# Token table instead of sorted rows: gathers by a one-hot table, RMS weights folded into the weights, half of W2 split in place

## The chip, the cores and the metric

The kernel runs on one core of a Trainium2 chip. The metric is the device time of one execution in microseconds (us); lower is better. The engines are TensorE (PE, with its weight loads as PEld), VectorE (DVE), ScalarE (ACT), GpSimd (POOL) and SyncE (SP), which here only issues DMAs.

## The reference

```python
# x (32, 112, 256), ctx (32, 375, 256), all float32; 16 heads of depth 16
x = x + xattn(ctx, ctx, layernorm(x), mask, wq, wk, wv, wo)
x = x + ffn(layernorm(x))
def ffn(x):                                   # 8 experts, hidden size 1024, top-1
    xn = x * rsqrt(mean(x * x) + 1e-6) * rms_w
    scores = softmax(xn @ gate_w.T)
    top1_idx, top1_score = argmax(scores), max(scores)
    for e in range(8):
        h = silu(xn @ W1[e] + b1[e]); ye = h @ W2[e] + b2[e]
        out = where(top1_idx == e, ye, out)
    return out * top1_score
```

## The kernel before

There are 32 batches of 112 query rows. **Attention** is a pipeline over batches. In step s the engines work on batch s (scores and row maxima), s-1 (transposed scores, exponentials, values), s-2 (output projection, residual, statistics of the second layernorm), s-3 (normalised row, gate) and ahead on s+1 and s+2 (context transposed, keys, queries). `run_steps` writes out steps -1 to 3, loops over steps 4 to 29 two at a time, and writes out 30 to 34; every engine has its own copy of this order and meets the others at semaphores.

SP issues all plain DMAs in one queue. In step s, for batch b = s: wait for `scoresT_ready` and `k_spilled`; four loads of `k_stack`; wait for `q_spilled`; four of `q_stack`; `load_batch(b+2)` (two of ctx, one of x); x again for the residual (`x_tail`); the spill of `w2_split`; loads of the next chunks of W1 and W2; the spills of keys and, after `q_parts_ready`, of queries for b+1; the spill of `x1` (batch b-2) to `x1_rows`.

VectorE has in a step four quads of row maxima (`row_maxima`, L1315) and between them, in this order: keys' low halves, division of heads, `centre` (L1338), `queries_stats(b+2)` (L1297, L1299, which waits for x of b+2), normalised queries (L1331), queries' low halves, `add_residual` with the second statistics (L1356 to L1360), context's low halves.

GpSimd has in a step: `split_w1` (L519 to L522: scale a 128x512 chunk by 256, round to float16, keep the remainder), `scale_routed` (L539, L540: the centred row times the RMS weights, once for TensorE and once into `xr_all`; waits for `centre`), `queries_rstd(b+2)` (L507, L509; waits for L1299), `split_w2` (L529 to L532), `residual` (L557), `mask_queries(b+1)` (L550, two), and `routed_factor` (L571, seven operations on 112x1: the layernorm and RMS factors of batch b-2). TensorE transposes `xr_now` (L1049) and makes the gate logits (L1058); ScalarE copies them out (L764).

`arena_a` holds attention's tiles and, after it, all of W2 in two float16 parts; so each split chunk of W2 goes to DRAM (`w2_spill`), and 8 DMAs of 1 MB load it back when attention ends.

**Routing** (from L1418). VectorE runs a chain of 35 links, each waiting for the one before: maximum, softmax, one-hot of the first maximum, ranks and counts by two float32 matmuls (L1137, L1139), a scan over batches, slot of each token, expert of each tile of 128 slots (`tile_expert`). GpSimd makes constants by iota and cast (L605 to L630). Then GpSimd issues 32 indirect DMAs (L636) that scatter the rows of `xr_all` (256 values, score, token number) to `sorted_rows`, which a 4.5 MB DMA had cleared at the start (L389).

**FFN**, 35 tiles of 128 slots: SP loads a tile's sorted rows (L464) and its expert's b2 (L468), PE transposes them (L1152), ACT and DVE split them in two float16 parts, PE computes the hidden layer (L1163, 48 matmuls), ACT applies silu (L831), DVE splits (L1497, L1500), PE computes outputs (L1178, 24 matmuls), DVE adds b2 and the residual (L1510, L1516), for which GpSimd gathered rows of `x1_rows` by token number (L649; the number comes from L1479), and GpSimd scatters the result to the output (L655). PE's order is transpose(t+1), hidden(t), outputs(t-1). Four buffers hold rows; the rows of tile t+4 may be loaded when `out_ready` of tile t has come.

## Time and the profile before

| | |
|---|---|
| median of 3 runs | 1008.66 us (1007.75 to 1008.96) |
| profiled execution, own time | 1013.72 us |
| its span | 1012.0 us |
| PE, PEld busy | 849.3, 612.3 us |
| DVE, ACT, POOL busy | 613.6, 448.0, 523.5 us |
| DMA | 143.72 MB, mean 142 GB/s |

The span is what the trace covers; all times of rows are from its start. A share of busy time is a mean over stages with different limits, so it is read stage by stage. A matmul's end is modelled, and GpSimd's spans are rough.

### The profile page before, as it was taken

How to read it: one execution, taken by the hardware profiler on the slowest of the kernel's cores; microseconds unless marked ns; L12 is line 12 of the kernel's file. 1: busy time of each engine (PE TensorE's matmuls, PEld its weight loads, DVE VectorE, ACT ScalarE, POOL GpSimd, SP SyncE). 2: the span in 40 equal slices, each digit the busy share in tenths (PEclk: the TensorE clock that was granted, in tenths of full speed). 3: DMA queues.
4: the chain of work that ended last, by engine and by line, in shares of the span. 5: the costliest groups of instructions: out<-in, count | busy, mean ns of one | idle time of the engine just before them, and what ended most of it. 6: DMA issues, size and time to landing. Idle time of an engine off the chain costs nothing.

```text
span 1012.0 us, 31886 instructions
## 1 busy us (share of the span) xinstructions
PE 849.3 (84%) x9355; PEld 612.3 (61%) x9356; DVE 613.6 (61%) x1906; ACT 448.0 (44%) x1121; POOL 523.5 (52%) x766
## 2 busy tenths in 40 slices
PE   1789999999999999999999999930089999999995
PEld 0456666666666666666666666610077777778773
DVE  4467777777777777777777777441044444445442
ACT  0235555555555555555555555500033333334331
POOL 0355567567667667667667667436622222232221
PEclk9999999999999999999999999955589999999998
DMA  9746765775775775775775775345222122222210
GB/s 255 184 131 164 188 185 160 179 195 149 185 200 147 187 201 144 185 206 142 189 204 142 187 206 144 76 194 215 87 58 72 59 63 76 58 71 71 66 48 7
DMA packets 124528, 143.72 MB, mean 142 GB/s; under 512 B 13274, under 2 KB 116550, under 8 KB 123464
## 3 DMA queue, kind: packets, MB, share of 16 engines
q1 hardware_dynamic: 119048, 132.15, 48.6%
q0 software_dynamic: 4896, 11.05, 3.4%
q8 instruction: 23, 0.38, 0.2%
q14 instruction: 17, 0.14, 0.0%
q10 hardware_dynamic: 544, 0.00, 0.0%
HBM read 100.10 MB, written 44.89 MB: 143 GB/s over the span
## 4 chain that ended last, share of the span: by engine, by line
PE 32%; issue 18%; SPq 15%; DMA 13%; POOL 12%; DVE 6%; ACT 1%; POOLq 0%; DVEq 0%; ACTq 0%
PE ps L1163 13%; DMA arena_a<-in_x 12%; PE ps L1178 10%; SPq L404 4%; SPq L399 4%; POOL arena_a L550 3%; POOL arena_b L529 3%; POOL arena_b L530 3%; PE ps L980 2%; POOL arena_a L557 2%; POOL arena_b L509 1%; SPq L365 1%; PE ps L994 1%; DVE arena_b L1297 1%; SPq L444 1%
## 5 line engine op out<-in xcount | busy, mean ns | idle before, releaser
L1315 DVE CUSTOM_DVE_ANT_0 arena_a<-ps,arena_a 112x375 bf16<-112x375 f32 x256 | 140.5, 549 | 45.5 <-PE ps L916 38.3
L697 ACT ACTIVATE arena_a<-ps 119x448 f32<-119x448 f32 (+1 forms) x256 | 131.7, 540 | 71.9 <-PE ps L942 71.3
L1163 PE MATMUL ps<-arena_b,w_parts 128*128 128x128 f16 x1680 | 148.5, 227 | 5.3 <-issue 4.3
L938 PE MATMUL ps<-arena_a 128*128 128x448 bf16 x384 | 137.3, 357 | 8.0 <-DVE arena_a L1324 5.9
L1163 PEld LDWEIGHTS ps<-arena_b,w_parts 128*128 x1680 | 118.7, 98 | 37.2 <-issue 11.2
L1315 DVE CUSTOM_DVE_ANT_0 arena_b<-ps,arena_a 112x375 bf16<-112x375 f32 x256 | 139.8, 546 | 0.0
L942 PE MATMUL ps<-arena_a 128*128 128x224 f16 x768 | 136.8, 260 | 0.0
L831 ACT ACTIVATE arena_b<-ps,b_sb 128x128 f32<-128x128 f32 x280 | 79.4, 372 | 113.3 <-PE ps L1163 113.1
L655 POOL DMA_INDIRECT out<-arena_b x35 | 35.6, 1018 | 179.8 <-DVE arena_b L1479 131.2
L1497 DVE TENSOR_SCALAR arena_b<-arena_b 128x512 f16<-128x512 f32 x70 | 30.3, 433 | 129.2 <-ACT arena_b L831 91.4
L1178 PE MATMUL ps<-arena_a,arena_b 128*128 x840 | 97.5, 273 | 4.6 <-DVE arena_b L1500 3.8
L942 PEld LDWEIGHTS ps<-arena_a 128*128 128x128 f16 x768 | 75.4, 98 | 39.9 <-issue 0.8
L1178 PEld LDWEIGHTS ps<-arena_a,arena_b 128*128 128x128 f16 x840 | 79.3, 98 | 17.5 <-issue 6.6
L697 ACT ACTIVATE arena_b<-ps 128x448 f32<-128x448 f32 x128 | 66.1, 541 | 49.2 <-PE ps L942 49.1
L994 PE MATMUL ps<-arena_a,arena_b 128*128 128x256 f16 x576 | 80.8, 278 | 5.3 <-DVE arena_a L1315 4.7
L539 POOL TENSOR_TENSOR arena_b<-arena_b,arena_a 112x256 f32<-112x256 f32 x32 | 20.5, 640 | 124.6 <-DVE arena_b L1338 124.6
L980 PE MATMUL ps<-arena_b,arena_a 128*128 128x375 f16 x384 | 76.3, 339 | 2.0 <-DVE arena_b L1276 1.2
L956 PE MATMUL ps<-arena_a,arena_b 128*17 128x112 f32 (+1 forms) x2048 | 74.0, 261 | 0.0
L550 POOL TENSOR_TENSOR arena_a<-arena_a 128x448 f16<-128x448 f16 x64 | 65.5, 1045 | 0.9 <-ACT arena_a L721 0.8
L994 PEld LDWEIGHTS ps<-arena_a,arena_b 128*128 128x128 f16 x576 | 51.7, 99 | 22.8 <-DVE arena_a L1315 14.6
L1282 DVE SCALAR_TENSOR_TENSOR arena_a<-ps,arena_a 128x375 f16<-128x375 f32 x64 | 39.0, 610 | 42.1 <-ACT arena_a L713 42.1
L916 PE MATMUL ps<-arena_a 32*112 32x375 f16 x512 | 48.6, 368 | 18.6 <-DVE arena_a L1282 10.1
(170 smaller groups left out, 1510.0 us busy)
## 6 DMA issues: line engine op xcount, KB each, us to landing
arena_a<-k_spill SPq DMA_DIRECT2D x128, 192.0 KB, 3.8
arena_b<-in_L_ffn_W SPq DMA_DIRECT2D x64, 256.0 KB, 4.3
arena_a<-q_spill SPq DMA_DIRECT2D x128, 112.0 KB, 4.4
k_spill<-arena_a SPq DMA_DIRECT2D x32, 384.0 KB, 4.7
arena_b<-in_ctx SPq DMA_DIRECT2D x32, 256.0 KB
w_spill<-arena_b SPq DMA_DIRECT2D x32, 256.0 KB, 4.5
arena_a<-w_spill SPq DMA_DIRECT2D x8, 1024.0 KB, 11.7
arena_a<-in_x SPq DMA_DIRECT2D x64, 112.0 KB, 4.6
```

The costliest lines, as they stand in the source:

```text
L550: pool.tensor_tensor(q_parts[par][:, part], q_split[:, part].unsqueeze(2).to_broadcast([P, DT, 2, T]), rows, ALU.mult).then_inc(q_parts_re ...
L697: nc.scalar.activation(probsT[u % PROB_BUFFERS][0:n], scoreT_bank[c][0:n, 0:QUAD * T], ACT.Exp, scale=1.0 / SCALE_SCORES).then_inc(probs_r ...
L831: last = nc.scalar.activation(h_act[:, f, :], ps[:, 1 + 2 * parity + f // 4, (f % 4) * P:(f % 4 + 1) * P], ACT.Silu, bias=b1_sb[:, bass.ds ...
L916: mm = pe.matmul(shared_bank[r][0:T, 0:S], q_parts[par][rows, 0, j, a, :], k_parts[par][rows, 0, j, 0:S], start=True, stop=True)
L938: pe.matmul(bank[:, 0:QUAD * T], mask_keys[:, quad, c, :], max_rows[par].rearrange("p h t -> p (h t)"), start=True, stop=False)
L942: mm = pe.matmul(bank[:, 2 * i * T:2 * (i + 1) * T], k_stack[par][:, r, j, c * P:(c + 1) * P], q_stack[par][:, r, j].rearrange("p a t -> p ...
L956: mm = pe.matmul(out_bank[32 * r:32 * r + VW, quad * T:(quad + 1) * T], v_aug[par][0:n, c, QUAD * quad + r, :], probsT[u % PROB_BUFFERS][0 ...
L980: mm = pe.matmul(proj_bank[j][:, 0:S], wk_parts[:, w_part, k, j * P:(j + 1) * P], ctx_parts[par][:, c_part, k, 0:S], start=k == 0 and n == ...
L994: mm = pe.matmul(bank[:, (c % 2) * D:(c % 2 + 1) * D], ctx_parts[par][:, c_part, k, c * P:(c + 1) * P], wv_parts[:, w_part, k, :], start=k ...
L1163: mm = pe.matmul(ps[:, 1 + 2 * parity + f // 4, (f % 4) * P:(f % 4 + 1) * P], w1_parts[:, w_part, bass.ds(e, 1), k, f * P:(f + 1) * P].rea ...
L1178: mm = pe.matmul(ps[:, 5 + parity, 0:D], h_parts[parity][:, h_part, f, :], w2_parts[:, w_part, bass.ds(e, 1), f, :].rearrange("p o d -> p ...
L1315: nc.vector.tensor_tensor_reduce(out=masked_scores[r % 2], in0=shared_bank[r][0:T, 0:S], in1=mask_bias, scale=-1.0, scalar=3.4e38, op0=ALU ...
```

## The change

Rows. `centre` now writes `row_tile[:, 0:D]` beside x1 in `row_tile[:, D:]`, and SP spills the pair (2 KB a row) in the step of batch b-3 to `rows`, laid out [T, B, 2D]. The sorted rows, the zeros and the scatter are gone: VectorE computes for every tile a list of its 128 tokens, and GpSimd gathers row pairs and scores by it (two indirect DMAs a tile). The list comes from TensorE: for each batch a 112x128 one-hot of the place in the tile, times token and batch number in the tile's column, summed over batches in PSUM. GpSimd's code for the FFN is written out, gather(t) ahead of scatter(t-4).

Factors. The two normalisations become one factor (variance plus a constant, power -0.5), and the RMS weights are multiplied into W1's scale and the gate weights at setup. Half of W2 (batches 0 to 15) is split straight to its place in `arena_w`; the other half is spilled and loaded back in four DMAs. Constants of routing are made by GpSimd inside the pipeline's step 32. SP's loop over steps becomes two (from 5 to 16 and from 17 to 28), GpSimd's too (from 4 to 15 and from 16 to 29).

```diff
-                if st.exists(2):
-                    wait_apart(sp, x1_ready, st.batch(2) + 1, sp_passed)
-                    sp.dma_start(x1_rows[bass.ds(st.batch(2), 1)].rearrange("o t d -> t (o d)"),
-                                 x1[st.parity(2)]).then_inc(x1_spilled[st.parity(2)], 16)
-            run_steps(sp, step)
+                if st.exists(3):
+                    wait_apart(sp, centred_ready, st.batch(3) + 1, sp_passed)
+                    sp.dma_start(rows[:, bass.ds(st.batch(3), 1), :].rearrange("t o d -> t (o d)"),
+                                 row_tile[st.parity(3)]).then_inc(rows_spilled[st.parity(3)], 16)
+            run_steps(sp, step, PEELED_FIRST + 1, DIRECT + 1)
...
-                scale = w_scale.to_broadcast([P, W_CHUNK])
+                scale = w1_scale[:, bass.ds(st.half(0), 1)].to_broadcast([P, W_CHUNK])
...
-                wait_count(pool, w2_spilled, 16 * b)
+                if st.base >= DIRECT:
+                    pool.wait_ge(w2_spilled, 16 * (b - DIRECT + 1))
+                    parts = [w2_split[:, part, :] for part in range(2)]
+                else:
+                    parts = [w2_chunks[:, bass.ds(b, 1), part, :].rearrange("p o n -> p (o n)") for part in range(2)]
...
-                for k, a0, a1, op in ((0, mv2[:, 1:2], eps_ln, ALU.add),
-                                      (1, ln2[:, 0:1], minus_half, ALU.pow),
...
+                pool.tensor_tensor(var2, mv2[:, 1:2], eps_two, ALU.add).then_inc(ln2_var, 1)
+                pool.wait_ge(ln2_var, b + 1)
+                pool.tensor_tensor(ln2, var2, minus_half, ALU.pow).then_inc(ln2_rstd, 1)
...
+                if not st.in_loop and st.base == B:
+                    route_constants()
...
-            for b in range(B):
-                pool.indirect_dma_start(out=sorted_rows, out_offset=bass.IndirectOffsetOnAxis(ap=slot_of[:, b:b + 1], axis=0),
-                                        in_=xr_all[:, b, :], in_offset=None).then_inc(scattered, 16)
...
+            pool.wait_ge(route, R_TOKENS)
+            def gather(t):
+                buffer = t % FFN_UNROLL
+                if t >= FFN_UNROLL:
+                    pool.wait_ge(out_ready, t - FFN_UNROLL + 1)
+                pool.indirect_dma_start(out=xs[buffer], out_offset=None, in_=rows.rearrange("t b d -> (t b) d"),
+                                        in_offset=token(t, 0), bounds_check=B * T - 1, oob_is_err=False
+                                        ).then_inc(xs_loaded[buffer], 16)
+                pool.indirect_dma_start(out=score[buffer], out_offset=None,
+                                        in_=score_rows.rearrange("t (b o) -> (t b) o", o=1),
+                                        in_offset=token(t, 0), bounds_check=B * T - 1, oob_is_err=False
+                                        ).then_inc(score_loaded[buffer], 16)
...
+            for t in range(FFN_TILES + FFN_UNROLL):
+                if t < FFN_TILES:
+                    gather(t)
+                if t >= FFN_UNROLL:
+                    scatter(t - FFN_UNROLL)
...
-                pe.wait_ge(xr_ready, 2 * b + 1)
+                pe.wait_ge(centred_ready, b + 1)
...
+            for b in range(B):
+                pe.wait_ge(places_ready, b + 1)
+                mm = pe.matmul(token_bank[:, 0:2 * FFN_TILES], at_place[:, b, :],
+                               in_tile_of[:, b].rearrange("p s n -> p (s n)"), start=b == 0, stop=b == B - 1)
...
+            link(nc.vector.tensor_tensor(in_tile, tile_base[:, :].unsqueeze(1).to_broadcast([T, B, FFN_TILES]),
+                                         slot_base.unsqueeze(2).to_broadcast([T, B, FFN_TILES]), ALU.is_equal))
+            link(nc.vector.tensor_scalar(in_tile_of[:, :, 0], in_tile, token_no[:, :], None, ALU.mult))
+            link(nc.vector.tensor_tensor(in_tile_of[:, :, 1], in_tile,
+                                         batch_no[:, :].unsqueeze(2).to_broadcast([T, B, FFN_TILES]), ALU.mult))
+            assert done[0] == R_TILES
+            for b in range(B):
+                nc.vector.tensor_scalar(at_place[:, b, :], place_no[:, :], place[:, b:b + 1], None, ALU.is_equal
+                                        ).then_inc(places_ready, 1)
+            dve.wait_ge(tokens_found, 1)
```

VectorE's chain is now 32 links and the 32 masks. `link` increments `route` and waits for it. It reaches the one-hot after 5 links (`R_ONEHOT`), the counts' copy after 6, the tile columns after 22 (`R_TILES`), the token list after 28 (`R_TOKENS`), `tile_expert` after 32 (`N_ROUTE`). TensorE makes counts (two bf16 matmuls) after link 5 and ranks (three) after link 6. The one-hots, counts, masks and columns are bf16. FFN matmuls, their order and the number of tiles are the same.

## Rows read from the trace of the kernel before

**Rows 1.** The page: its first line.

```profile
span 1012.0 us, 31886 instructions
```

**Rows 2.** Windows by stage: busy us per engine, clock, DMA share, GB/s.

```profile
62.00:648.00 586.00, 548.66 (x6474) 375.88 (x6472) 440.56 (x1461) 334.05 (x759) 390.74 (x600) 1.00 0.67 174
...
670.00:735.00 65.00, 3.34 (x9) 1.70 (x8) 13.64 (x46) 0.98 (x3) 36.21 (x48) 0.50 0.54 195
```

**Rows 3.** Chain that ended last, attention: start, us, what; first and last of 19.

```profile
218.80 4.97 DMA arena_a<-in_x
...
561.52 4.87 DMA arena_a<-in_x
```

**Rows 4.** Waits from 100 to 600 us: waiter, releaser, total, times, longest.

```profile
POOL arena_b L539 <- DVE arena_b L1338: 105.7, 26, 4.4
...
DVE arena_b L1297 <- DMA arena_a<-in_x: 39.0, 26, 2.2
...
POOL w_parts L522 <- POOL w_parts L520: 4.8, 26, 0.2
```

**Rows 5.** Timeline of one attention step: start, us, engine, line, operation.

```profile
490.98 0.19 POOL L507 TENSOR_TENSOR arena_b<-arena_b,arena_a 112x1 f32<-112x1 f32 x1 [0.42 <-DVE arena_b L1299]
...
497.75 0.36 SPq L439 DMA_DIRECT2D q_spill<-arena_a  x1
...
504.53 0.33 SPq L369 DMA_DIRECT2D arena_a<-in_x  x1
```

**Rows 6.** Window of one microsecond ahead of the stack loads' flow.

```profile
500.00:501.00 1.00, 1.00 (x9) 0.69 (x9) 1.00 (x5) 0.51 (x2) 0.51 (x2) 1.00 0.55 138
```

**Rows 7.** Timeline of the end of attention.

```profile
664.03 0.82 POOL L571 TENSOR_TENSOR arena_b<-arena_b,arena_a 112x1 f32<-112x1 f32 x2 [1.97 <-DVE arena_b L1360]
...
666.67 0.41 DVE L1338 TENSOR_SCALAR arena_b<-arena_b 112x256 f32<-112x256 f32 x1 [2.78 <-POOL arena_b L571]
...
668.04 0.61 PE L1049 MATMUL ps<-ident,arena_b 112*128 112x112 f32 x2 [3.67 <-POOL arena_b L539]
...
670.04 0.18 ACT L764 ACTIVATE gate_logits<-ps 112x8 f32<-112x8 f32 x1 [1.00 <-PE ps L1058]
```

**Rows 8.** Timeline of routing and of the scatters.

```profile
670.25 0.42 DVE L1418 TENSOR_REDUCE arena_b<-gate_logits 112x32 f32<-112x256 f32 x1 [3.17 <-ACT gate_logits L764]
670.29 0.45 POOL L605 IOTA arena_b<- 128x256 int32 x1 [1.80 <-ACT gate_logits L764]
...
677.38 0.42 DVE L1434 COPY arena_b<-ps 112x256 f32<-112x256 f32 x1 [2.27 <-PE ps L1139]
...
680.67 0.23 DVE L1440 COPY arena_b<-arena_b 128x128 f32<-128x128 f32 x1
680.82 0.28 DVE L1441 TENSOR_TENSOR arena_b<-arena_b 128x128 f32<-128x128 f32 x1
...
686.91 0.17 DVE L1469 TENSOR_SCALAR tile_expert<-arena_b 1x35 int32<-1x35 f32 x1
687.38 1.19 POOL L636 DMA_INDIRECT sorted_rows<-xr_all,slot_of  x1 [13.00 <-DVE tile_expert L1469]
...
726.33 0.94 POOL L636 DMA_INDIRECT sorted_rows<-xr_all,slot_of  x1 [0.30 <-issue]
```

**Rows 9.** Timeline of the start of the FFN.

```profile
734.34 0.69 PE L1152 MATMUL ps<-ident,arena_b 128*128 128x128 f32 x2 [2.63 <-DMA arena_b<-sorted_rows]
...
735.31 5.29 PE L1163 MATMUL ps<-arena_b,w_parts 128*128 128x128 f16 x48 [0.28 <-issue]
```

**Rows 10.** DMA issues: queue, count, KB each, us to landing.

```profile
arena_a<-w_spill SPq DMA_DIRECT2D x8, 1024.0 KB, 11.7
...
arena_b<-x_rows,arena_b POOLq DMA_INDIRECT x35, 2.9
```

**Rows 11.** Timeline of one tile of the FFN.

```profile
974.33 0.48 DVE L1516 SCALAR_TENSOR_TENSOR arena_b<-arena_b 128x256 f32<-128x256 f32 x1
...
981.56 0.38 PE L1152 MATMUL ps<-ident,arena_b 128*128 128x128 f32 x2
```

More of the change, by code:

```diff
@@ L35 @@
 FFN_TILES = (B * T + EXPERTS * (P - 1)) // P
+DIRECT = B // 2
 GROUPS = ((0, 0), (0, 1), (1, 0), (1, 1))
@@ L129, in carve @@
                 n *= d
+            n += n % 2
+            if which == "a" and used["a"] + n > arena_a.shape[1]:
+                which = "b"
             at = used[which]
-            used[which] += n + n % 2
-            assert used[which] <= arena.shape[1]
+            used[which] += n
+            arena = arena_a if which == "a" else arena_b
+            assert used[which] <= arena.shape[1], (which, used)
+            n = 1
+            for d in shape:
+                n *= d
             flat = arena[0:parts, at:at + n]
@@ L204, in build @@
         attT = carve("b", P, DT, T)
-        x1 = [carve("b", T, D) for _ in range(2)]
-        centred = carve("b", T, D)
-        xr_now = carve("b", T, D)
         xrT = carve("b", P, DT, T)
@@ L1412, in over_experts @@
             def over_experts(ap):
[L1413 to L1416 removed]
+                return ap.unsqueeze(1).to_broadcast([T, EXPERTS, B])
             dve.wait_ge(gate_copied, B)
[L1418 to L1419 removed]
```

516 lines of the change are left out of this document (256 added, 260 removed).

## The prediction

> **What bounds the kernel now.** I read the stage windows first [rows 2], then the chain of waits, then timelines of the pieces it names. The span of the profiled execution is 1012.0 us [rows 1], its own time 1013.72, the median of the runs shown 1008.66; I work in the span and carry the difference over to the median unchanged. A difference under 0.2% (2 us) counts as none. There are three stages, each with its own limit.
>
> Attention, to about 648 us: TensorE is busy 548.66 of 586 us [rows 2], yet the chain goes through the load of x. It landed last in 18 steps between 218.80 and 561.52, 342.7 us or 19.04 a step [rows 3]. VectorE waits for x in each of the 26 steps of the window, 39.0 us in all [rows 4], and its third quad of row maxima, on which TensorE waits, stands behind that. One step [rows 5]: GpSimd begins the variance of x at 490.98 and runs without a pause through W2's split, the residual and the masking of queries; SP then issues the query spill at 497.75, the x1 spill, eight stack loads, two context loads and x at 504.53. With the landing (4.87 in one step [rows 3]) this loop of SP, DMA, VectorE and GpSimd closes at 18.9 to 19.1. GpSimd's 4 us wait for the centred rows (105.7 us [rows 4]) lies before that point and limits nothing.
>
> Routing, 670 to 735 us: TensorE does 3.34 us of work in 65, at a granted clock of 0.50 (1.2 GHz) [rows 2]. VectorE routes from 670.25 to 687.08; 32 scatters issue from 687.38, the last at 726.33 [rows 8]; sorted rows are read back and hidden(0) starts at 735.31 [rows 9]. The FFN behind is TensorE's own work and only moves with its start.
>
> **The change, part by part.**
>
> *End of attention.* In the last step the factor took seven GpSimd operations from 664.03, the centring began at 666.67, the first routed transpose at 668.04, the last gate copy ended at 670.22 [rows 7]. Now it takes two operations, the 0.82 us pair of the first row: centring can begin at 664.96, 1.7 earlier. TensorE then reads VectorE's output without the two GpSimd products: centring ends 0.41 after its start, so 0.96 us lay between, and about 0.15 remains. Together 2.5: routing starts at 667.75.
>
> *Route constants.* 36 GpSimd operations enter the first step after the last split. A 256-element iota takes 0.45 and its cast begins 0.52 after it [rows 8]; at 0.2 to 0.5 each I estimate 12 us. GpSimd's products and five factor operations have gone, and VectorE and TensorE are busy there with batches 30 and 31; factor and residual of those are needed about 13 us on. I cost it at nothing. If it were 5 us longer, the centring of batch 30 and with it the tail would be 3 us late.
>
> *VectorE's chain to the token table* (R_TOKENS, 28 links). A 256-element link costs 0.42 + 0.04, a small one 0.17 + 0.03 [rows 8]. Five links to the one-hot 2.3. TensorE's two counting matmuls, in bf16: the old float32 pair left VectorE idle 2.27 [rows 8], a bare handover costs some 0.3; nearer the low end, since the passes are fewer, 0.85. Copy 0.46. Ranks, three longer matmuls in the same bounds: 1.3. Tiles, starts and slots: three at 0.2, two at 0.25, three at 0.46, 2.5. Slot to tile: 0.9. Three operations over 1120 elements a partition: 0.17 plus 1.05 ns an element (the slope between the 1x35 and 112x256 links) is 1.35; 1.38 with the link for the two with two tensors, 0.8 for the scalar one (0.75 to 1.38). Then 32 place masks of 128 elements, each with its own matmul: the nearest row is the 128-element copy, after which the next operation starts 0.15 later [rows 8], so 4.8, plus 0.3 for the last matmul; bounds 0.11 (3.5 in all) and 0.5 (16). Six small ones 1.3. The sum 18.2 against 16.8 before: the table is ready at 686.0. The four links that follow (expert of each tile) and the scores' way out hide behind the gathers.
>
> The Trainium skill ("VectorE: DVE Perf Modes", What auto-detection actually checks) says that a one-source operation on 16-bit tensors in SBUF runs in the 4x mode. No row here shows a bf16 pair; by that rule masks come at the lower spacing, and the time would be about 2 us less than by the row.
>
> *Scatter and read-back go, gathers come.* GpSimd starts 0.30 after its release, and further indirect DMAs follow 1.25 to 1.35 apart [rows 8]. Hidden(0) stands behind transpose(1), whose rows are the third indirect DMA (rows 0, score 0, rows 1): 686.3 + 2.6 = 688.9. A gather lands in 2.9 [rows 10]; 2 KB rows for 1 KB, +0.3: 692.1. Then 0.97 as before [rows 9]: hidden(0) at 693.1, against 735.31: 42.2 us earlier, the 2.5 included. Bounds of this sum: 37 (both matmul waits 2.27, scalar operations at one element a cycle) to 46. Two waits are new: SP waits for the scores (ready some 4.5 us into VectorE's chain) with the W2 reload and the b2 loads queued behind, and GpSimd for the scores' spill with the gathers behind; both are over some 10 us before the table. The W2 reload is four 1 MB transfers instead of eight, issued before the table; eight landed in 11.7 us each at the median [rows 10], and outputs(0) needs them only some 9 us after hidden(0). Nothing.
>
> *FFN.* GpSimd has three indirect DMAs a tile, some 4 us of a period of 7.4. The gather of a tile is released by the output four tiles back, ready at 974.81; the transposes that would need it come a tile later, at 981.56 [rows 11]. With 0.14 + 1.0 + 3.2 it lands with 2.4 us left. VectorE loses 0.15 us a tile that hides under TensorE. Nothing; without the cover each microsecond of lateness would cost 31.
>
> *The attention loop.* Removed: two products, five factor operations, 16 W2 spills. None is in the cycle: the spill is issued behind x on SP, the products stand before the wait. So no gain. Three things lengthen it. (1) In the direct steps the split writes to an address from a register: the like store of W1 waits 4.8/26 = 0.18 us [rows 4], W2's store is too short of a wait to be in that list: +0.1 in 12 looped steps, 1.2 (0 to 2.2). (2) The row spill is 224 KB for 112, queued between query spill and stack loads. In the microsecond before the loads flow, DMA is 0.55 busy [rows 6], so most fits into the gap; 112 KB at that row's 138 GB/s is 0.8 us, less the idle 0.45: at most some 0.4, at least 0. I take 0.1 in 29 steps, 2.9. (3) SP has two loops to enter instead of one. 0.5.
>
> The Trainium skill ("Runtime: NRT & Kernel Launch", Instruction fetch mechanics) says a taken branch out of the fetched window stalls the engine. No row above isolates it; it gives no figure for a loop entry.
>
> *Setup.* Two small VectorE operations ahead of the weights, 0.4, less one 112 KB broadcast; the 4.5 MB of zeros goes, on which nothing critical waited. +0.2.
>
> Sum: -42.2 + 1.2 + 2.9 + 0.5 + 0.2 = -37.4. Span 974.6; median 1008.66 - 37.4 = 971.3.
>
> **Rivals.**
> A. The cycle of x takes the full 0.4 to 0.5 us a step, through the doubled spill and its 64 KB stride: 29 x 0.35 more, 981.5. For it: no slack on that path [rows 3]. Against: the gap [rows 6].
> B. The table is slow: mask, semaphore and matmul pair at 0.3 to 0.5 us instead of 0.15, 5 to 11 more: 976 to 982. For it: 32 handovers at TensorE's lower clock. Against: VectorE doesn't wait between them.
> C. The bf16 operations run at the fast end (masks 3.5, long ones halved: -3.8) and the loop loses nothing (-4.6): 963.
> D. Slower than before: the loop stretches. The saving of 42 is used up when each of 29 steps is over 1.45 us longer, for instance if the strided row writes took 0.3 us each instead of fitting the gap (7 to an engine). Time then 1012 and up. Against: the 1 KB W2 spill writes have strides of the same kind, and end within the step.
> E. No change: row gathers late in every tile by 1.2 us. Speaks against it the 2.4 us left.
>
> **Chances.** Forecast 0.69 (its own range 966 to 977), A 0.10, B 0.08, C 0.10, D 0.02, E 0.01. Range 963 to 982: it takes in C, A and most of B. Faster 0.97, same 0.01, slower 0.02.
>
> **What would show it.** Two GpSimd operations and one centring between the last statistics and the last transposes, and the last gate copy some 7 us after those statistics instead of 9; VectorE's chain from the first routing operation to the last token operation 18 us (17 to 21); 32 masks 0.15 apart; first gather 0.3 behind; hidden(0) 25 us after the last gate copy; then 277 us to the end, as before. Steps of 19.0 to 19.3 in the loop. The prediction is wrong if the steps move by over 0.3 either way, if the table is nearer 30 us, or if TensorE waits for gathered rows in the loop of tiles.

## The result, and the profile after

The changed kernel takes 973.47 us at the median of four runs (972.89 to 974.91), the kernel before 1008.4 on the same chip: ratio 0.9656, 95% interval 0.9639 to 0.9673, 34.9 us less. On a second chip the medians are 973.46 and 1010.22, ratio 0.9636 (0.9614 to 0.9658). The prediction was 971.3, in the range 963 to 982.

That the total came out near the forecast is luck: it hides errors of opposite sign. The stages up to the last gate copy became 8.0 us shorter where 2.3 longer was forecast, those behind it 32.7 shorter where 39.7 was forecast. Each kernel was profiled twice; the stages are read from the starts of the score matmuls, the last gate copy, hidden(0) and the last output in the timelines (us, first and second trace; the difference is that of the means):

| stage | before | after | difference | predicted |
|---|---|---|---|---|
| start to step 5 | 136.5, 138.0 | 133.3, 135.0 | -3.1 | +0.2 |
| steps 5 to 31 | 495.1, 495.5 | 492.0, 492.5 | -3.0 | +4.6 (29 steps, entry) |
| step 31 to the last gate copy | 38.7, 38.4 | 36.9, 36.5 | -1.9 | -2.5 |
| last gate copy to hidden(0) | 65.1, 64.4 | 27.5, 27.5 | -37.3 | -39.7 |
| hidden(0) to the last output | 266.2, 266.1 | 270.8, 270.4 | +4.4 | 0 |
| last output to the end | 10.4, 10.4 | 10.6, 10.6 | +0.2 | 0 |

The traces differ by 40.7 us, the medians by 35 to 37, since both profiled executions of the kernel before were 3 to 5 us over its medians (1013.72 to 1008.4, 1014.69 to 1011.83), those of the kernel after within 1 (972.89 and 974.21). In each of four sets of its runs, the executions with a listed mean clock of 0.955 and more were on average 1.4 to 2.2 us longer than the rest, and both profiled ones (0.957 and 0.958) are of that kind; what else makes up the 3 to 5 us is open. The first line of the page after, for [rows 1]:

```profile
span 971.1 us, 31136 instructions
```

The windows after, for [rows 2]: busy us per engine, clock, DMA share, GB/s:

```profile
62.00:640.00 578.00, 544.61 (x6433) 372.19 (x6431) 436.82 (x1455) 332.64 (x754) 310.00 (x395) 1.00 0.66 174
662.00:690.00 28.00, 8.08 (x45) 4.80 (x46) 18.15 (x67) 1.36 (x4) 7.55 (x8) 0.50 0.52 188
```

GpSimd has lost some 80 us of work in attention and TensorE is as busy as before; routing is 28 us for 65, still at a granted clock of 0.50, the lower level. The end of attention, for [rows 7]:

```profile
658.58 0.19 POOL L583 TENSOR_TENSOR arena_b<-arena_b,arena_w 112x1 f32<-112x1 f32 x1 [5.87 <-DVE arena_b L1400]
658.85 0.56 POOL L585 TENSOR_TENSOR arena_b<-arena_b,arena_w 112x1 f32<-112x1 f32 x1
...
659.44 0.41 DVE L1378 TENSOR_SCALAR arena_w<-arena_w,arena_b 112x256 f32<-112x256 f32 x1 [1.00 <-POOL arena_b L585]
...
660.00 0.61 PE L1071 MATMUL ps<-ident,arena_w 112*128 112x112 f32 x2 [1.08 <-DVE arena_w L1378]
...
662.00 0.18 ACT L786 ACTIVATE gate_logits<-ps 112x8 f32<-112x8 f32 x1 [1.00 <-PE ps L1080]
```

Two GpSimd operations, the centring 0.86 us behind the start of the first (2.64 in [rows 7]), TensorE 0.15 behind the centring's end, as forecast. Routing and the first gathers, for [rows 8, 9]:

```profile
662.22 0.42 DVE L1457 TENSOR_REDUCE arena_b<-gate_logits 112x32 f32<-112x256 f32 x1 [2.36 <-ACT gate_logits L786]
...
665.41 0.39 DVE L1466 CAST arena_b<-ps 128x224 bf16<-128x224 f32 x1 [0.59 <-PE ps L1160]
...
670.34 1.33 DVE L1489 TENSOR_TENSOR arena_b<-tile_base,arena_b 112x1120 bf16<-112x1120 bf16 x1
671.70 0.53 DVE L1491 TENSOR_SCALAR arena_b<-arena_b,token_no 112x1120 bf16<-112x1120 bf16 x1
...
673.62 0.58 DVE L1496 TENSOR_SCALAR arena_b<-place_no,arena_b 112x128 bf16<-112x128 bf16 x3
...
680.38 0.20 DVE L1507 SCALAR_TENSOR_TENSOR arena_b<-arena_b 128x35 uint32<-128x35 f32 x1
...
681.63 1.29 POOL L676 DMA_INDIRECT arena_b<-rows,arena_b  x1 [17.91 <-DVE arena_b L1511]
...
684.53 1.00 POOL L676 DMA_INDIRECT arena_b<-rows,arena_b  x1 [0.30 <-issue]
...
688.72 0.69 PE L1187 MATMUL ps<-ident,arena_b 128*128 128x128 f32 x2 [2.52 <-DMA arena_b<-rows,arena_b]
...
689.69 4.33 PE L1198 MATMUL ps<-arena_b,w_parts 128*128 128x128 f16 x48 [0.28 <-issue]
```

VectorE's chain to the table took 18.36 us (662.22 to 680.58; 18.2 forecast), the 32 masks 5.3. The first gather begins 1.05 us behind the table, not 0.30, and the transposes of rows(1) start 4.2 after their gather, not 3.2. The DMA issues, for [rows 10]:

```profile
arena_w<-w_spill SPq DMA_DIRECT2D x4, 1024.0 KB, 8.1
arena_b<-rows,arena_b POOLq DMA_INDIRECT x35, 3.5
```

### The profile page after: what moved, and what is told of

It is laid out like the page before. It is cut to its first block, busy times and chain, and to the rows that moved or that the text cites. A ratio compares the mean times of both kernels' runs of the same rounds, so it can differ in the third digit from the quotient of the medians.

```text
span 971.1 us, 31136 instructions
## 1 busy us (share of the span) xinstructions
PE 851.8 (88%) x9388; PEld 610.6 (63%) x9389; DVE 619.2 (64%) x1895; ACT 449.1 (46%) x1122; POOL 453.0 (47%) x564
## 4 chain that ended last, share of the span: by engine, by line
PE 47%; POOL 11%; DMA 10%; SPq 10%; issue 10%; DVE 9%; ACT 2%; POOLq 0%; DVEq 0%; ACTq 0%
PE ps L1198 14%; PE ps L1213 10%; DMA arena_w<-in_x 9%; POOL arena_w L570 4%; PE ps L1002 3%; SPq L443 3%; PE ps L1016 3%; SPq L438 3%; PE ps L960 3%; PE ps L978 2%; PE ps L964 2%; POOL arena_b L558 2%; PE ps L938 2%; POOL arena_w L559 2%; POOL arena_w L577 1%
## 5 line engine op out<-in xcount | busy, mean ns | idle before, releaser
L719 ACT ACTIVATE arena_b<-ps 128x448 f32<-128x448 f32 (+1 forms) x384 | 194.2, 541 | 119.6 <-PE ps L964 118.8
L1356 DVE CUSTOM_DVE_ANT_0 arena_w<-ps,arena_w 112x375 bf16<-112x375 f32 x256 | 140.3, 548 | 48.7 <-PE ps L938 42.1
L960 PE MATMUL ps<-arena_b,arena_w 128*128 128x448 bf16 x384 | 137.2, 357 | 6.2 <-DVE arena_b L1365 5.6
L1356 DVE CUSTOM_DVE_ANT_0 arena_b<-ps,arena_w 112x375 bf16<-112x375 f32 x256 | 139.5, 545 | 0.1
L964 PE MATMUL ps<-arena_b 128*128 128x224 f16 x768 | 136.7, 260 | 0.0
L1213 PE MATMUL ps<-arena_w,arena_b 128*128 x840 | 97.7, 273 | 4.8 <-DVE arena_b L1536 3.4
L978 PE MATMUL ps<-arena_b 128*17 128x112 f32 (+1 forms) x3072 | 100.4, 261 | 0.3
L1213 PEld LDWEIGHTS ps<-arena_w,arena_b 128*128 128x128 f16 x840 | 78.9, 98 | 18.6 <-issue 7.1
L1016 PE MATMUL ps<-arena_w,arena_b 128*128 128x256 f16 x576 | 80.8, 278 | 4.3 <-DVE arena_w L1356 3.4
L1002 PE MATMUL ps<-arena_b,arena_w 128*128 128x375 f16 x384 | 75.6, 337 | 2.0 <-DVE arena_b L1317 1.2
L1016 PEld LDWEIGHTS ps<-arena_w,arena_b 128*128 128x128 f16 x576 | 51.7, 99 | 21.2 <-DVE arena_w L1356 13.5
```

The source lines that it names most:

```text
L719: nc.scalar.activation(probsT[u % PROB_BUFFERS][0:n], scoreT_bank[c][0:n, 0:QUAD * T], ACT.Exp, scale=1.0 / SCALE_SCORES).then_inc(probs_r ...
L960: pe.matmul(bank[:, 0:QUAD * T], mask_keys[:, quad, c, :], max_rows[par].rearrange("p h t -> p (h t)"), start=True, stop=False)
L964: mm = pe.matmul(bank[:, 2 * i * T:2 * (i + 1) * T], k_stack[par][:, r, j, c * P:(c + 1) * P], q_stack[par][:, r, j].rearrange("p a t -> p ...
L978: mm = pe.matmul(out_bank[32 * r:32 * r + VW, quad * T:(quad + 1) * T], v_aug[par][0:n, c, QUAD * quad + r, :], probsT[u % PROB_BUFFERS][0 ...
L1002: mm = pe.matmul(proj_bank[j][:, 0:S], wk_parts[:, w_part, k, j * P:(j + 1) * P], ctx_parts[par][:, c_part, k, 0:S], start=k == 0 and n == ...
L1016: mm = pe.matmul(bank[:, (c % 2) * D:(c % 2 + 1) * D], ctx_parts[par][:, c_part, k, c * P:(c + 1) * P], wv_parts[:, w_part, k, :], start=k ...
```

## The experiments

All ratios are to the kernel before, timed beside them; its medians there lay between 1010.2 and 1011.8. The diffs show the lines that matter; "..." marks what is left out. Where a step or a stage is given, it is read from the profiled execution.

**A second trace of before.** No edit.

> The kernel before, profiled a second time. Its first profiled execution had an own time of 1013.72 us, 5 above the median 1008.4. If those 5 us lay in the stretch before the first step's scores and in the steps of the second half (theory: the trace of before was a long one there), this trace shows step 16 starting about 344 instead of 347 us and step 31 about 628 instead of 631.5, and the loop gained little by the change. Rival: this execution takes 1008 and is as long as the first one in the steps (19.0 in both halves), and the 5 us lay elsewhere.

1014.69 us in the profiled run. Step 5 starts at 138.0, steps 5 to 16 take 19.14 on average, 17 to 28 19.06: as in the first trace, and step 16 starts at 348.5, not at 344. The rival holds in what it says of the steps: the first trace was no freak there, and the changed kernel's second half (18.79) is really shorter. Its 1008 us didn't come: this execution too is over the median.

**Zeros put back.**

```diff
+            sp.dma_start(sorted_rows.rearrange("(n p) d -> p n d", p=P),
+                         zeros.unsqueeze(1).to_broadcast([P, FFN_TILES, D + 2])).then_inc(zeroed, 16)
...
+            pool.memset(zeros, 0.0).then_inc(constants, 1)
```

> The kernel after with the 4.5 MB write of zeros put back where it was (its result is not used). Theory 1: that write competed with the loads of the first steps; step 1's scores start about 59.5 instead of 56.7 us, and the time is 976 to 976.5, some 2.8 above 973.5. Theory 2 (my prediction's): nothing critical waits for it, the first step's 2.8 us come from elsewhere; 973.5, within 0.5.

975.68 us, ratio 0.9651 (0.9625 to 0.9677); step 1 starts at 57.3 (56.7 and 58.8 in the two traces of the kernel after), so the write costs nothing at the start, as predicted. But in the steps 17 to 28 it took 18.95 for 18.79, and GpSimd's subtraction of the split 1160 ns for 1090. The tile `zeros` had moved the tiles behind it by 1032 bytes. Whether the one follows from the other, this run doesn't show; it led to the sweep below.

**Seven GpSimd operations put back.**

```diff
+                for n in range(5):
...
+                    pool.tensor_tensor(spare_row[:, n:n + 1], eps_two, eps_ln, ALU.add).then_inc(spare, 1)
+                for n in range(2):
...
+                    pool.tensor_tensor(spare_row, bvo, bvo, ALU.mult).then_inc(spare, 1)
```

> The kernel after with seven GpSimd operations of the sizes of the removed ones put behind the factor in each step (five of one column, two of 112x256; their results are not used). Theory: their removal shortened the loop's GpSimd chain or took load off the port that VectorE shares; with them the steps behind the direct half go back from 18.7 to 19.0, the direct half from 19.1 to 19.3, and the time is 977 to 980. Rival (the prediction's 'none is in the cycle'): steps unchanged, the tail at most 3 us later, 973.5 to 976.

974.59 us, ratio 0.963 (0.961 to 0.965), steps 17 to 28 18.83. The rival holds, the prediction's "none is in the cycle": the removed products and factors gave the loop nothing that stands out from the difference between two traces of one kernel.

**Half the row spill.** The centred halves in DRAM are filled once, with x, so the FFN computes on other numbers with the same instructions.

```diff
+            sp.dma_start(rows[:, :, 0:D], x.rearrange("b t d -> t b d")).then_inc(filled, 16)
...
-                    sp.dma_start(rows[:, bass.ds(st.batch(3), 1), :].rearrange("t o d -> t (o d)"),
-                                 row_tile[st.parity(3)]).then_inc(rows_spilled[st.parity(3)], 16)
+                    sp.dma_start(rows[:, bass.ds(st.batch(3), 1), D:].rearrange("t o d -> t (o d)"),
+                                 row_tile[st.parity(3)][:, D:]).then_inc(rows_spilled[st.parity(3)], 16)
```

> The kernel after with a row spill of the residual half alone, 112 KB a step instead of 224; the centred halves of the rows in DRAM are filled once, during the first steps, with x (the FFN's input is replaced by x). My prediction put 0.1 us a step on the doubled spill: then 2.9 us less than the kernel after, 970.6, or a ratio to before of 0.963, and steps 0.1 shorter in both halves. Rival A of the prediction: 0.4 to 0.5 a step, 0.952. Theory 3: the doubled spill fits the gap before the stack loads and costs nothing: ratio 0.9656, steps as in the kernel after (19.16 on average over steps 5 to 16, 18.8 over 17 to 28).

Steps 5 to 16 took 19.06 (19.16 and 19.25 in the two traces of the kernel after), 17 to 28 18.68 (18.79, 18.78). The 0.1 of the prediction agrees, though two traces of one kernel differ by as much in the first of these; rival A is out. Its total (973.08, 0.961) says little: the four executions took 970.0, 970.9, 975.2 and 977.2, and the longest, the profiled one, has an FFN 5 us longer than the kernel after's.

**All of W2 through the spill.**

```diff
-DIRECT = B // 2
+DIRECT = 0
...
-            run_steps(sp, step, PEELED_FIRST + 1, DIRECT + 1)
+            run_steps(sp, step)
```

> The kernel after with the direct half at nothing: all of W2 goes through the spill, 8 reload transfers instead of 4. Each tile that GpSimd touches keeps its position within 64 bytes. Theory P: the direct split costs 0.1 us of GpSimd's path a step (6.65 against 6.55 from the variance to the masked queries) and 0.35 of the period; without it steps 5 to 16 fall from 19.16 to 18.8, like those behind them, and the last gate copy is 4 us earlier. The reload then has only some 25 us from its issue at 660 to outputs(0): 8 MB at the 200 GB/s that the loads move take 40, and outputs(0) waits about 15 us for them, so that the whole is slower than the kernel after, 985. Rival: steps unchanged, so the half without W2 spills differs for another reason; and reload in time, 973.

981.84 us, ratio 0.9702 (0.9675 to 0.9729). GpSimd's path from the variance to the masked queries is 6.54 us in every step, as theory P says (6.65 in the direct half of the kernel after), but the steps take 19.12 and 19.14, so theory P's price for the direct half is wrong, at least as this run tests it: the edit also takes SP's and GpSimd's loops back to their one entry, so that the second half (18.79 before the edit) changed by it too. Outputs(0) did not wait for the reload: it starts 10.0 us behind hidden(0) in both. The reload held up the rows instead. Window of the gathers in this kernel:

```profile
684.00:697.00 13.00, 1.93 (x10) 1.14 (x11) 2.91 (x11) 0.77 (x2) 8.28 (x8) 0.50 0.99 385
```

With the DMA engines at 0.99, rows(1) took 6.5 us from gather to transposes for 4.2, and hidden(0) came 2.3 later. This is what the direct half gives here.

**No score gathers.** The outputs are scaled with a column of the identity.

```diff
-                pool.indirect_dma_start(out=score[buffer], out_offset=None,
-                                        in_=score_rows.rearrange("t (b o) -> (t b) o", o=1), ...
...
-                nc.vector.scalar_tensor_tensor(out=out_rows[buffer], in0=y_sb, scalar=score[buffer],
+                nc.vector.scalar_tensor_tensor(out=out_rows[buffer], in0=y_sb, scalar=ident[:, 0:1],
```

> The kernel after without the 35 score gathers (the outputs are scaled by a column of the identity instead of the score). Theory S: the third indirect DMA of each tile is what makes three of four tiles 0.2 us longer than before (it delays the loading of TensorE's instructions or the reading of the expert number); from hidden(0) to the end 276.7 as in the kernel before, and rows(1) come 1.3 earlier: ratio 0.9596, some 6 us less than the kernel after. Rival W: TensorE's new addressing of W2 costs it; then the tiles stay at 281.4, and only the 1.3 us are won, 972.

970.02 us, ratio 0.9592 (0.9562 to 0.9622). Theory S falls: from hidden(0) to the last output 270.2, as in the kernel after (270.8, 270.4). What was won lies behind the last output (7.8 us for 10.6), where no engine computes any more. The 1.3 us were not won either: rows(1), gathered second instead of third, landed 5.9 us after their gather.

**A gather ahead, and a sweep of tile positions.** One execution, 1061.38 us with the sweep behind the last output.

```diff
...
+            pool.indirect_dma_start(out=warm_row, out_offset=None, in_=rows.rearrange("t b d -> (t b) d"), ...
...
+            for moved in range(3):
+                for shift in range(0, 16, 2):
+                    at.shift = [shift if k == moved else 0 for k in range(3)]
+                    then(pool.tensor_tensor(at(2, D, T), at(0, D, T), at(1, D, T), ALU.add))
```

> The kernel after with two additions. (1) One indirect gather of rows 0 to 127, not used, on GpSimd while the token table is made. Theory: the first indirect DMA after a long pause loads GpSimd's code, which is why the first gather came 1.05 us after the table and not 0.30; then the first real gather comes 0.3 behind and hidden(0) 0.75 earlier. Rival: 1.05 is what a gather's release costs, unchanged. (2) Behind the last output, a sweep: GpSimd's split subtraction, residual addition and query masking, each 24 times, with one operand at a time moved by 8 bytes over 64. Theory B: the durations that changed between the kernels (subtraction 1158 to 1090 ns, masks 1045 to 977, residual 638 to 729) follow from the tiles' positions; the sweep shows the same steps of about 70 and 90 ns. Rival: position does nothing (all within 10 ns) and the durations changed by what ran beside them. The span is about 75 us longer by the sweep.

The first real gather starts 0.88 after the table for 1.05 and takes 1.01 us for 1.29, so 0.45 of the delay has to do with its being the first; the rest stays. Later releases cost less: in the loop of tiles GpSimd starts a gather 0.80 us behind the output that frees its buffer. Hidden(0) gained nothing (27.6 behind the last gate copy): rows(1) took 4.7 from their gather. The sweep, six single operations of its timeline: subtraction, addition, masking, each with both sources at multiples of 16 bytes, then with one source 8 bytes further:

```profile
976.10 1.15 POOL L726 TENSOR_TENSOR arena_w<-arena_w 128x512 f16<-128x512 f32 x1
977.34 1.08 POOL L726 TENSOR_TENSOR arena_w<-arena_w 128x512 f16<-128x512 f32 x1
1005.41 0.72 POOL L730 TENSOR_TENSOR arena_w<-arena_w 112x256 f32<-112x256 f32 x1
1006.21 0.64 POOL L730 TENSOR_TENSOR arena_w<-arena_w 112x256 f32<-112x256 f32 x1
1032.93 1.04 POOL L734 TENSOR_TENSOR arena_w<-arena_w 128x448 f16<-128x448 f16 x1
1034.05 0.98 POOL L734 TENSOR_TENSOR arena_w<-arena_w 128x448 f16<-128x448 f16 x1
```

Moving on by 8 bytes each time alternates between the two: the subtraction 1152, 1081, 1153, 1092, 1152, 1090, 1152, 1092 ns with its first source moved, the addition 723, 641, 723, 640, 723, 640, 722, 638 (635 to 639 with the second moved), the masking 1042, 977, 1038, 973, 1040, 975, 1038, 972 with its second. The other source, moved in its turn, changes nothing for the subtraction (1152 to 1155) and the masking (1037 to 1044), and nor does the output (within 3 ns). Theory B holds.

**The kernel after again**, as the base for the last versions.

> The kernel after, unchanged, on the same chip as the three that follow and as a second trace of it: 973.5 us, or a ratio of 0.963 to 0.966; from the last gate copy to hidden(0) 27.5 us, from there to the last output 270.8, steps 19.2 in the direct half and 18.8 behind it.

As expected in every stage (table above); its start to step 5 took 1.7 us more than in the first trace.

**W1 in the order of W2.**

```diff
-        w1_parts = sb("w1_parts", [P, 2, EXPERTS, DT, F], F16)
+        w1_parts = sb("w1_parts", [P, EXPERTS, 4, 2, W_CHUNK], F16)
...
-                                           w1_parts[:, w_part, bass.ds(e, 1), k, f * P:(f + 1) * P
+                                           w1_parts[:, bass.ds(e, 1), 2 * k + f // 4, w_part, f % 4 * P:(f % 4 + 1) * P
```

> The kernel after with W1 stored in the same order as W2 (expert, chunk, part), nothing else. With one order for both the adds come back: tiles of 7.06, from hidden(0) to the last output 4 to 5 us less, 969. Rival: the gather queue or VectorE sets the 7.24, nothing changes, 973.5.

967.25 us, ratio 0.959 (0.9568 to 0.9611), 6.2 less than the kernel after. Hidden(0) to the last output 267.5. The chains that ended last, one tile each, of the kernel after and of this one:

```profile
757.52 4.18 PE ps L1198 x48
761.71 2.78 PE ps L1213 x24
764.49 0.22 PE ps L1187 x2
764.71 0.13 issue
764.84 4.18 PE ps L1198 x48
```

```profile
784.87 4.07 PE ps L1198 x48
788.94 2.76 PE ps L1213 x24
791.70 0.22 PE ps L1187 x2
791.92 3.11 PE ps L1198 x36
```

The matmuls are the same; the 0.13 "issue" between transposes and hidden units is gone. Of the loop's four kinds of tile two last 7.06 to 7.15 us for 7.25 to 7.37, one 8.33 for 8.51, one is as it was. In the trace of TensorE's sequencer the outputs of four tiles have 48 ALU_OP and 16 FUSED_REGOPS for their addresses in the kernel before, 64 FUSED_REGOPS in the kernel after, and 48 and 16 again here. Theory W holds for 3 of the 4.4 us; the rest of the 6.2 lies ahead of the FFN.

**A version meant to beat both.** Beside the W1 order:

```diff
-                    for n, (w_part, h_part) in enumerate(PASSES):
-                        mm = pe.matmul(ps[:, 5 + parity, 0:D], h_parts[parity][:, h_part, f, :],
+                    for h_part in ((1, 0) if f == FT - 1 else (0, 1)):
+                        n = D if h_part else 2 * D
+                        mm = pe.matmul(ps[:, 5 + parity, 0:n], h_parts[parity][:, h_part, f, :],
+                                       w2_parts[:, bass.ds(e, 1), f, 0:n].rearrange("p o d -> p (o d)"),
...
-            transpose_rows(1, 1, 0, False)
-            hidden(0, expert_of(0), 0, True)
+            hidden(0, expert_of(0), 0, True, lambda: transpose_rows(1, 1, 0, False))
...
+        carve("a", T, 2)
```

> A version meant to beat both. On the kernel after: (1) the two parts of a W2 row side by side, so that one address serves both and the high part of the hidden units is multiplied with 512 columns at once: 16 matmuls and 8 addresses for the outputs of a tile instead of 24 and 16; VectorE adds the two halves; W1 in the same order; (2) hidden(0) begins ahead of the transposes of tile 1, which come in its middle; rows of tiles 0 to 2 are gathered ahead of the scores; Silu's table is loaded during the routing; (3) two words of padding that put the residual's two sources 8 bytes apart. If TensorE's sequencer is what bounds the FFN, as its trace says (32 addresses x 0.124 + 16 x 0.124 + 1.2 for the expert's number and the waits = 7.2), a tile falls to about 6.2 and the FFN by 28 to 31; (2) gives 3 to 4, (3) 0.09 a step, 1 to 2.5: 936 to 942. If TensorE's array bounds it, only (2) and (3) show: 968.

949.1 us, ratio 0.9395 (0.9379 to 0.9412): 24 less than the kernel after, though not the 936 to 942 expected. FFN 253.3 for 270.6, last gate copy to hidden(0) 25.1 for 27.5, residual 637 ns for 729, steps 17 to 28 18.68. Two tiles of its chain:

```profile
784.98 3.39 PE ps L1224 x48
788.37 2.74 PE ps L1240 x16
791.11 0.22 PE ps L1211 x2
791.33 0.38 issue
791.71 4.21 PE ps L1224 x48
795.92 0.09 issue
796.01 2.77 PE ps L1240 x16
```

In every other tile the 48 matmuls of the hidden units now run in 3.4 us instead of 4.2; the others start behind 0.4 to 0.6 us of issue and still take 4.2. In the 3.4 us tiles the sequencer's first address stands 0.7 us ahead of the first matmul, in the others 0.1. The outputs stay at 2.7 us with 16 matmuls as with 24, for the same number of columns, so no instruction bound them.

The sequencer has lost its lead by a wait. It worked out its last address at 803.04 and passed the wait for gathered rows only at 804.95, 0.03 us behind their landing, and those rows had been asked for late:

```profile
800.04 0.48 DVE L1583 SCALAR_TENSOR_TENSOR arena_b<-arena_b 128x256 f32<-128x256 f32 x1 [0.24 <-DVE arena_b L1576]
...
801.33 1.02 POOL L689 DMA_INDIRECT arena_b<-rows,arena_b  x1 [4.02 <-DVE arena_b L1583]
...
805.04 0.44 PE L1211 MATMUL ps<-ident,arena_b 128*128 128x128 f32 x2
```

The output frees the buffer at 800.52, the gather starts 0.80 later, and its rows are there 3.6 us behind that. Such stands of 1.4 to 2.0 us come in every fourth tile, and in 18 of the 28 tiles from 4 to 31 the sequencer passes that wait within 0.05 us of the landing; in the kernel after it comes 0.9 to 2.6 us behind it. So the gathers with their four buffers bind this version beside the sequencer. That fits a gain of 17 instead of 28; a version with more buffers, which would show it, was not run.

**SP's loop one step later, in the kernel before.**

```diff
...
-            run_steps(sp, step)
+            run_steps(sp, step, PEELED_FIRST + 1)
```

> The kernel before, with SP's loop of two steps entered one step later, as the change had to do it for its two loops; the work is the same. The trace of before shows 0.32 us more between query spill and key loads in every second step, where SP's loop branches back; the change moved that to the other kind of step. Theory SP: with the branch in the odd steps x is in time there; steps fall from 19.05 to 18.8, 1008 becomes 1001. Rival: no change, 1008, and the 0.25 us a step that the kernel after gains in its second half comes from GpSimd's shorter operations (tile positions) alone.

1008.95 us, ratio 0.9989 (0.9974 to 1.0003), steps 17 to 28 19.03. The 0.32 us more moved with the loop's entry to the other kind of step. The steps 17 to 28 stayed; the steps 5 to 16 took 18.99 for 19.15 and 19.14, and from step 5 to 31 this trace is 3.0 us shorter than those of the kernel before. Theory SP falls with its 7 us; 1 to 3 us are not excluded.

**Padding alone, in the kernel before.** Three lines, 24 bytes a partition.

```diff
...
+        carve("a", P, 2)
         pair_keep = carve("a", P, 2, T)
+        carve("a", P, 2)
...
         w_scale = carve("b", P, 1)
+        carve("b", P, 2)
```

> The kernel before with three paddings of two words (8 bytes) and nothing else: one ahead of pair_keep, one behind it, one ahead of the staging tiles of the weight split. By the sweep GpSimd's masks fall from 1045 to 977 ns, its two split subtractions from 1160 to 1090, the residual stays at 638; from the variance of x to the masked queries 6.67 becomes 6.46. Theory B: that path is the cycle through x, so steps 5 to 28 fall from 19.1 to 18.85 or 18.9, 5 to 6 us over 29 steps, ratio 0.994 to 0.996; the 0.12 us that the changed kernel gained there by its tile positions is then worth about 3 us of its loop. Rival: TensorE fills the gap or x lands no earlier, so that the steps stay at 19.05 to 19.15; ratio 0.999 to 1.001.

999.88 us, ratio 0.9873 (0.9853 to 0.9893): 11.4 us less, twice what was expected. GpSimd's operations over ten steps, of before and then of this kernel:

```profile
L550 POOL TENSOR_TENSOR arena_a<-arena_a 128x448 f16<-128x448 f16 x20 | 20.5, 1046 | 0.0
...
L532 POOL TENSOR_TENSOR arena_b<-arena_b 128x512 f16<-128x512 f32 x10 | 11.6, 1163 | 0.8
```

```profile
L553 POOL TENSOR_TENSOR arena_a<-arena_a 128x448 f16<-128x448 f16 x20 | 19.0, 971 | 0.0
...
L535 POOL TENSOR_TENSOR arena_b<-arena_b 128x512 f16<-128x512 f32 x10 | 11.1, 1108 | 0.8
```

Its waits from 100 to 600 us, for [rows 4]:

```profile
DVE arena_b L1300 <- DMA arena_a<-in_x: 6.5, 13, 1.4
```

VectorE's wait for x falls from 39.0 us to 6.5, and the steps from 19.1 to 18.66. They alternate between 18.3 to 18.4 and 18.9, and the third quad of maxima stands at one place in each kind of step (10.45 to 10.56 and 10.78 us behind the step's first scores; in the kernel before 10.5 to 11.7). The steps of a kind now agree to 0.01 us and TensorE is busy in 172.5 of 180 us for 169: it seems to have become the bound, though no run tests that by itself.

## Why the prediction was right, and where not

**End of attention: right** (-1.9 for -2.5). The factor gave 1.78 us for 1.7 and the products the 0.8; the rest of the stretch, the same work in both kernels, is 0.7 longer, where traces of one kernel differ by 0.3 to 0.4. One sign of the forecast was misread: the last gate copy "some 7 us after those statistics instead of 9". From the first factor operation to the end of that copy it was 6.2 us, as [rows 7] show, and is 3.6.

**Route constants: right.** They ended at 651.1 in the kernel after and the centring of batch 30 was not late.

**Table: right**, by terms that erred both ways: masks 5.3 for 4.8, first counting matmuls' wait 0.59 for 0.85, scalar operation over 1120 bf16 elements 0.53 for 0.8, the two with two tensors 1.33 for 1.35. The Trainium skill ("VectorE: DVE Perf Modes", What auto-detection actually checks) has the one-source operation at four times the rate; the rows agree in kind but not in size (0.53 against 1.33; 0.36 against 1.16 without the 0.17 of a small operation, 3.2 times), and masks of 128 elements gain nothing from it: 0.165 apart, where my row said 0.15.

**Gathers: 2 us too short.** The release took 1.05 for 0.30, the third indirect DMA started 2.9 after the first for 2.6, and its rows landed in 4.2 for 3.2. That the first indirect DMA is longer was measured (0.45 of it, by the gather ahead). What sets the landing of rows(1) is open: gathered second, or 0.3 earlier, they came 8.1 to 8.6 us behind the table all the same. With the reload doubled they were later still, so "W2 reload: nothing" held only because half of W2 had its place already. SP's two b2 loads, which start in between, were not taken away. In the loop of tiles the terms 0.14 + 1.0 + 3.2 were wrong one by one and right in their sum: the release costs 0.80 and the landing 3.5 from the issue on.

**FFN: the step that failed.** "The FFN is TensorE's own work" held, and TensorE never waited for gathered rows: its sequencer came to that wait 0.9 to 2.6 us behind their landing, for the 2.4 us of the forecast. What I didn't look at was the instructions between the matmuls. A tile of 7.06 us is 32 x 0.124 + 16 x 0.113 = 5.8, and about 1.3 us for the expert's number and waits: the sequencer bounds it. The branch of the loop stands in the tile of 8.33. In the kernel before W1 and W2 had their experts the same 2048 elements apart, and an address of W2 was one of W1's plus a constant; the change moved W2's to 4096. 16 x 0.011 = 0.18 us in three of four tiles. Undoing that alone by W1's order gave back 3.1 of 4.4 us. Of the other 1.3, 0.5 lie in tile 4 (7.83 us for 7.32 and 7.23 in the traces of before), where the sequencer stood 0.65 us at the wait for the rows of tile 6, which landed 5.1 us after their gather; the rest is open.

**The loop: sign wrong.** My three additions were 4.6 us, and it lost 3.0. Steps of 19.0 to 19.3 were the sign, and the second half's 18.8 is outside it. The address store is there: GpSimd's path is 6.65 us in the direct half and 6.55 behind it. The doubled spill agrees with 0.1. A second entry of SP's loop was not measured by itself. The term I didn't have is the position of tiles. The change rearranged both arenas; the subtractions fell from 1163 to 1092 ns and the masks from 1045 to 977, the residual rose from 638 to 729, in all -0.12 us on the path that closes through x.

A second thing goes with the steps. VectorE's normalised queries of 112x256 (one source, `normalize_queries`) take 0.41 us by themselves. But where they start while GpSimd rounds W2's chunk to float16, the second operation of its split, they last until that ends. Of the kernel before and then of the padded one:

```profile
474.18 1.04 POOL L530 TENSOR_TENSOR arena_b<-arena_b 128x512 f16<-128x512 f32 x1
...
474.28 1.09 DVE L1331 TENSOR_SCALAR arena_a<-arena_a,arena_b 112x256 f32<-112x256 f32 x1
```

```profile
461.51 1.04 POOL L533 TENSOR_TENSOR arena_b<-arena_b 128x512 f16<-128x512 f32 x1
...
462.40 0.41 DVE L1334 TENSOR_SCALAR arena_a<-arena_a,arena_b 112x256 f32<-112x256 f32 x1
```

In 14 traces, steps 5 to 28, the operation is longer than 0.43 us in 312 of 336 cases, and in all of them it ends 0.15 us behind that operation of GpSimd. The fifth and sixth columns have its mean (us). Over the kernels:

| kernel | GpSimd's path, first and second half | steps 5 to 16 | steps 17 to 28 | VectorE's operation, 5 to 16 | 17 to 28 |
|---|---|---|---|---|---|
| before, SP later | 6.67, 6.67 | 18.99 | 19.03 | 1.07 | 1.08 |
| before (two traces) | 6.67, 6.67 | 19.15, 19.14 | 19.05, 19.06 | 1.10, 1.06 | 1.06, 1.09 |
| after + zeros | 6.72, 6.61 | 19.26 | 18.95 | 1.08 | 1.06 |
| after (two traces) | 6.65, 6.55 | 19.16, 19.25 | 18.79, 18.78 | 1.06, 1.08 | 0.95, 0.97 |
| after, all spilled | 6.54, 6.54 | 19.12 | 19.14 | 1.06 | 1.09 |
| version to beat both | 6.55, 6.45 | 19.14 | 18.68 | 1.05 | 0.63 |
| before, padded | 6.47, 6.47 | 18.66 | 18.66 | 0.42 | 0.42 |

The padding moves tiles and does nothing else, and the steps fall to 18.66 with it. The path's length alone doesn't order the rows: at 6.54 the kernel with all of W2 spilled stays at 19.13 and the first half of the version to beat both at 19.14, where the second half of the kernel after has 18.79. VectorE's operation orders just these: in all 14 traces, each half in which it takes 1.04 us or more has steps of 18.95 to 19.28, at 0.94 to 0.98 they are 18.78 to 18.83, below 0.83 18.66 to 18.71. So the padding may act through its start as well as through the path. Which of the two is the cause and which follows from shorter steps was not tested by itself.

The stretch to step 5 is 3.1 us shorter; the zeros are not it. Part of it is TensorE's clock, which is another from trace to trace of one kernel, and no gain that can be put down to the change. In both traces of the kernel before and in the second of the kernel after a weight load of 128x128 in float16 takes some 147 ns until about 64 us and 98 behind that. The first trace of the kernel after has granted clocks of 0.93 from 40 to 44 us and 0.95 from 47 to 50, near the upper level of 2.4 GHz, and the short loads from 61.0; it reaches step 5 at 133.3 and the second at 135.0. The padded kernel, with a granted clock of 0.74 from 37 to 50, is there at 133.0. From 137.2 without such stretches to 135.0 without them, 2.2 us stay unexplained.

Of the rivals, A (0.35 a step) and B (slow table) did not occur, C's 963 was off by the gathers and the FFN, D and E are out. The forecast's own sign against itself, steps moving by over 0.3, was only just missed (-0.27 in the second half). The Trainium skill ("Runtime: NRT & Kernel Launch", Instruction fetch mechanics) has a taken branch stall the engine when its target is not in the fetched window. Here SP's loop costs 0.32 us more in every second step, and the 0.32 moved with the loop's entry; whether it is such a stall no run shows.

## What to carry to other kernels

Count the instructions between the matmuls, not only the matmuls: where weights are addressed by a register, a change of layout changes what an address costs, and a tile can be bound by it. Where GpSimd is in a cycle, look at its durations of the same operation in two kernels before explaining a step by waits: three paddings of two words were worth 1.3% here, a third of what the whole change brought. Look also at what VectorE does while GpSimd's operations run, and at how long it takes there. Look at the slack of every wait again when a bound is moved: with the sequencer relieved, the gathers came to bind. And check each stage by its length, one that "only moves" too, since a total can be right by errors that cancel, as this one.

## What was not expected of the hardware

GpSimd's operations with two sources alternate between two durations as one source moves by 8 bytes: 1152 and 1090 ns (128x512, split subtraction), 723 and 640 (112x256, float32 addition), 1041 and 975 (128x448, masking); the output's position does nothing. For the addition the slow case is both sources at the same offset in 16 bytes. VectorE's operation on 112x256 elements takes 0.41 us by itself; where it starts beside GpSimd's conversion of 128x512 to float16, it ends 0.15 us behind the end of that, and takes up to 1.09 us. TensorE's 48 matmuls of 128 columns and their 32 computed addresses take 4.2 us, and 3.4 where the addresses were worked out ahead. And three of the variants (all spilled, half the rows, the sweep) have an FFN of 275.6 to 276.1 us instead of 270.2 to 270.8, in the first of them by 0.4 to 0.85 us in each of seven tiles; the edits don't touch it. What differs is seen in the traces. In 20 to 23 of their 35 tiles the signal for the second half of the hidden units comes late to ScalarE, so that silu starts 1.0 to 2.7 us behind the end of the last matmul instead of 0.1 to 0.8. The output is then ready 1.6 to 3.2 us behind the outputs' matmuls instead of 1.05 to 1.29, the gathers are released later, and TensorE waits for gathered rows, which it never does in the kernel after: 1.2 us in four tiles with half the rows, 1.8 in three in the sweep, and with all of W2 spilled

```profile
PE ps L1187 <- DMA arena_b<-rows,arena_b: 0.7, 2, 0.5
```

Why the signal comes late is open. Since one variant's four executions range from 970.0 to 977.2 us, it may belong to the execution and not to the edit.
